# Transposes of the attention probabilities through single-pass float32 names

## The reference

```python
xn = _layernorm(x)
kv_c, q_c = xn @ W_kvd + b_kvd, xn @ W_qd + b_qd          # 64 and 192 wide
# keys and queries per head: 128 from kv_c/q_c, 64 more with a rotary embedding
scores = jnp.einsum('bhqd,bhkd->bhqk', q, k) * scale
scores = jnp.where(causal, -1e9, scores)
probs = jax.nn.softmax(scores, axis=-1)
ctx = jnp.einsum('bhqk,bhkd->bhqd', probs, values)
out = x + (ctx @ W_o + b_o) + ffn(xn)                     # ffn: one product with binarized weights
```

## Time and profile before

| | |
|---|---|
| three runs | 1427.53, 1427.95, 1428.28 us; median 1427.95 |
| the profiled execution, first to last instruction (span) | 1427.6 us |
| mean granted clock of TensorE over the span | 0.997 of full speed |
| DVE, ACT, POOL busy | 81%, 84%, 70% of the span |

### The profile page before, as it was taken

The page is one execution under the profiler, slowest core; times in us unless marked ns, Lnnn a source line. Parts: engine busy times, 40 slices in busy tenths (PEclk is TensorE's granted clock), DMA queues, the critical chain, the costliest instruction groups (busy, mean ns, idle before and its releaser), DMA issues.

```text
span 1427.6 us, 27603 instructions
## 1 busy us (share of the span) xinstructions
PE 1394.7 (98%) x9786; PEld 1262.8 (88%) x9786; DVE 1151.8 (81%) x2708; ACT 1203.2 (84%) x2603; POOL 998.3 (70%) x573
## 2 busy tenths in 40 slices
PE   6979999999999999999999999999999999999998
PEld 4769999998899999988899999999889999999987
DVE  4858898885788888887678889888677888888888
ACT  4658888997788988898788888899778988888887
POOL 6986777777667877768765777777766777666750
PEclk9999999999999999999999999999999999999999
DMA  9752212212343222211333222221233322221110
GB/s 269 226 126 50 73 50 64 64 49 64 75 106 81 79 64 64 64 44 36 78 93 96 68 68 63 64 64 49 64 75 90 87 58 65 64 63 47 36 27 31
DMA packets 46957, 106.82 MB, mean 75 GB/s; under 512 B 9333, under 2 KB 17830, under 8 KB 46822
## 3 DMA queue, kind: packets, MB, share of 16 engines
q1 hardware_dynamic: 43360, 94.01, 25.7%
q0 software_dynamic: 3296, 11.01, 2.7%
q10 hardware_dynamic: 166, 0.03, 0.0%
HBM read 48.92 MB, written 9.96 MB: 41 GB/s over the span
## 4 chain that ended last, share of the span: by engine, by line
PE 87%; ACT 6%; DVE 2%; SPq 1%; DMA 1%; POOL 1%; issue 1%; POOLq 0%; ACTq 0%; DVEq 0%
PE turn L1554 17%; PE ring L1499 11%; PE u_ps L1575 9%; PE ring L1531 9%; PE ring L1530 9%; PE u_ps L1576 9%; PE ring L1529 8%; PE o_ps L1599 4%; PE o_ps L1600 4%; PE ring L1512 2%; ACT probs L778 2%; PE ring L1438 2%; PE ring L1444 2%; ACT probs_hi L787 1%; DMA swapped<-k_rope 1%; POOL k_rope L367 1%
## 5 line engine op out<-in xcount | busy, mean ns | idle before, releaser
L1076 DVE TENSOR_SCALAR_CACHE_REDUCE probs<-ring,c_t 128x1024 f32<-128x1024 f32 (+7 forms) x512 | 414.3, 810 | 96.6 <-PE ring L1531 92.1
L1086 DVE TENSOR_TENSOR probs_lo<-turn,probs_hi 128x512 fp32r<-128x512 f32 (+1 forms) x640 | 401.2, 630 | 69.0 <-ACT probs_hi L787 64.1
L787 ACT ACTIVATE probs_hi<-turn 128x512 fp32r<-128x512 f32 (+1 forms) x640 | 349.7, 549 | 105.1 <-PE turn L1554 99.3
L778 ACT ACTIVATE probs<-probs,row_min 128x1024 f32<-128x1024 f32 (+7 forms) x512 | 394.3, 771 | 11.8 <-DVE probs L1076 9.2
L1554 PE MATMUL turn<-ident,probs 128*128 128x128 f32 x2304 | 387.2, 275 | 3.2 <-DVE probs_lo L1086 2.3
L1575 PE MATMUL u_ps<-probs_hi,kv_nat 128*128 128x256 f32 x1147 | 312.6, 302 | 1.0 <-DVE u_pair L1092 1.0
L1554 PEld LDWEIGHTS turn<-ident,probs 128*128 128x128 f32 x2304 | 282.9, 140 | 29.0 <-ACT probs L778 6.6
L1576 PE MATMUL u_ps<-probs_lo,kv_nat 128*128 128x256 f32 x1147 | 287.7, 280 | 0.0
L1529 PE MATMUL ring<-k_hi,q_hi 128*128 128x512 f32 (+3 forms) x768 | 275.4, 359 | 0.0
L1531 PE MATMUL ring<-k_hi,q_lo 128*128 128x512 f32 (+3 forms) x768 | 263.1, 343 | 0.0
L1530 PE MATMUL ring<-k_lo,q_hi 128*128 128x512 f32 (+3 forms) x768 | 262.5, 342 | 0.0
(11 more groups left out here) (229 smaller groups left out, 2582.9 us busy)
## 6 DMA issues: line engine op xcount, KB each, us to landing
swapped<-k_rope SPq DMA_DIRECT2D x128, 128.0 KB, 2.3
wv<-wv_scratch SPq DMA_DIRECT2D x62, 256.0 KB, 4.0
wp<-wp_scratch SPq DMA_DIRECT2D x62, 192.0 KB, 3.5
wp<-wp_scratch SPq DMA_DIRECT2D x31, 256.0 KB, 3.1
swapped<-q_y SPq DMA_DIRECT2D x62, 128.0 KB, 2.3
swapped<-q_x SPq DMA_DIRECT2D x62, 128.0 KB, 2.3
k_hi<-qb_kv_hi SPq DMA_DIRECT2D x16, 256.0 KB, 3.7
k_lo<-qb_kv_lo SPq DMA_DIRECT2D x16, 256.0 KB, 4.8
```

The costliest lines, as they stand in the source:

```text
L778: act.activation(p, p, ACT.Exp, scale=-1.0, bias=row_min[:, r:r + 1], accum_out=row_sum[:, g % 4, w, h:h + 1]).then_inc(exp_ready, 1)
L787: act.activation(probs_hi[:, r % 4, 0:width], turn[r % 2][:, 0:width], ACT.Identity).then_inc(turned_hi, 1)
L1076: dve.tensor_scalar(probs_of(g, w, h), ring[slot_of(entry)][:, KEY_COLUMN[qt]:KEY_COLUMN[qt] + keys], c_t[b % 2][:, qt, ds(pair * 2 + h, 1 ...
L1086: dve.tensor_tensor(probs_lo[:, r % 4, 0:width], turn[r % 2][:, 0:width], probs_hi[:, r % 4, 0:width].bitcast(F32), ALU.subtract).then_inc ...
```

## The change

The 2304 transposes at L1554 get all three operands in the single-pass float32 format. The probabilities get a second set of SBUF tensors with the same shape in that format, which lie where the first set lies: the first set is given back to the allocator at once, and the second takes its room. DVE and ACT go on writing and reading the first names, PE reads the second. The identity is made as a tensor of the single-pass format, and all its other users read a float32 view of it. The PSUM banks `turn` keep their type for ACT and DVE; the transposes write them through a view. No bytes, waits, loops or orders are changed.

```diff
-        ident, ident_bf, mask_bf = sb("ident", [P, P]), sb("ident_bf", [P, P], BF16), sb("mask_bf", [P, P], BF16)
+        ident_r, ident_bf, mask_bf = sb("ident", [P, P], F32R), sb("ident_bf", [P, P], BF16), sb("mask_bf", [P, P], BF16)
+        ident = ident_r[:, :].bitcast(F32)
...
-        probs = [[sb(f"probs{i}{h}", [P, (NT + 1) * P]) for h in range(2)] for i in range(2)]
+        with ExitStack() as plain:
+            probs = [[plain.enter_context(nc.sbuf_tensor(f"probs{i}{h}", [P, (NT + 1) * P], F32)) for h in range(2)] for i in range(2)]
+
+        probs_r = [[sb(f"probs_r{i}{h}", [P, (NT + 1) * P], F32R) for h in range(2)] for i in range(2)]
...
+        turn_r = [bank[:, :].bitcast(F32R) for bank in turn]
...
+        def probs_turned(g, w, h, kt):
+
+            long, short = LONG_SHORT[g % BLOCKS]
+            return probs_r[g % 2][h][:, ((long + 1) * w + kt) * P:][:, 0:P]
...
-            pool.affine_select(out=ident[:, :], in_=ident[:, :], compare_op=ALU.not_equal, fill=1.0, base=0,
+            pool.affine_select(out=ident_r[:, :], in_=ident_r[:, :], compare_op=ALU.not_equal, fill=1.0, base=0,
...
-                        mm = pe.transpose(turn[r % 2][:, (2 * t + h) * P:(2 * t + h + 1) * P],
-                                          probs_of(g, w, h)[:, kt * P:(kt + 1) * P], ident[:, :])
+                        mm = pe.transpose(turn_r[r % 2][:, (2 * t + h) * P:(2 * t + h + 1) * P],
+                                          probs_turned(g, w, h, kt), ident_r[:, :])
```

## The result

The changed kernel takes 1410.12 us (median of 4 runs, 1409.15 to 1411.24) against 1428.12 us (4 runs, 1427.53 to 1428.86) in the same comparison: ratio 0.9873, 95% interval 0.9859 to 0.9887. It is faster by 18 us; 62 were forecast. The profiled execution has a span of 1408.9 us, 18.7 less than before.

A forecast was written before the change was run, and what follows sets the result against it. PE was taken to bound the kernel, busy for 98% of the span. Cheaper transposes would free 122 us, less 39 for GpSimd's key chain and 21 for ACT: gain 62, time 1366 us, range 1335 to 1434.

The forecast's parts named there:

- price of the new transpose: PE's 2304 transposes at L1554: step from start to start falls from 0.108 to 0.055 us, 122 us in all.
- midway case: Transposes at 0.082 us each: PE loses 60 us; 1388 us with two thirds kept, 1408 with one third.
- tied to transposing and not to the format: Weight loads of transposes: the quick load, 140 against 189 ns, was inferred to stay in the new format, supporting 0.055 us.
- rival of the load: New-format transposes wait for weight loads, 0.110 to 0.115 us each: slower by 5 to 16 us, 1438 us; chance 0.20.
- decision point: Weight loads of the transposes: the change makes the kernel slower once a load lasts longer than 0.108 us.
- bounds 0.055 and 0.115: Limits on a new transpose's step in us: one pass from below, the single-pass format's weight load from above.
- GpSimd's key chain, 39 us lost: Chain for the next pair's keys, 12.8 of each pair's 39.8 us without slack: some 39 of 122 us lost.
- ACT as what is late next: ACT, close behind PE in the attention blocks, takes a quarter of the remaining 83 us: 21 us.
- busy floor of 181.5 us in 200: ACT in the stretch 1140 to 1340 us: 178.09 us busy plus 3.4 us of gaps, against PE falling to 180.8.
- give-back: Part of PE's 122 us lost again to other engines: 39 us to GpSimd's key chain, 21 us to ACT.
- queries' chain: GpSimd's second chain, before the scores: 4.1 us of slack against about 2.8 us gained by PE, so it holds.
- rival that the format changes nothing: Transposes at L1554 still move four bytes an element in two passes: 0 us gained, 1428 us; chance 0.15.

The follow-up runs named there:

- e9: Changed kernel with the cosine product of GpSimd's key chain done during the swap instead of after it: 1405.58 us, ratio 0.9832.
- e2: Changed kernel with GpSimd's rope operations cut to a quarter of their columns from the fourth projection on: 1406.55 us, ratio 0.9841.
- e12: Changed kernel with the fourth block's last exponential moved behind the second waiting group of the next pair: 1398.48 us, ratio 0.9779.
- e1: Separate kernel of TensorE alone, rows of 64 like instructions, nothing of the layer computed: transpose step 0.109 us old format, 0.085 new.

## Why the prediction was right in sign and wrong in size

- **The price of the new transpose** is the term that was mis-sized: taken as 0.055 us, measured as 0.085 in a row, and in groups of four as 0.091 with what the next matmul pays (the old 0.109 less 17 to 19 ns). 2304 x (0.108 - 0.055) = 122 us became 40 to 45. The prediction's own midway case, a price of 0.082, gave 1388 to 1408 us; the result is 1410.
- **How that choice was made.** The old step was right (0.108 against 0.1095), and so, it seems, was the one pass: the shortest new transposes last 222 ns. The inference from load durations, "tied to transposing and not to the format", held for the duration, which stays at 140, and failed for what it was used for: in the old format a load really is over in 0.063 us or less (L186), and the new one holds the load path for 0.085 under the same duration, although its matmul starts 0.03 us after the load. The sum needed the interval between two loads' starts, and no row of before had it for this format.
- **The rival of the load** named the right mechanism, a load that outlasts the pass, with the wrong number: 0.110 to 0.115, from score matmuls, would have made it slower. The decision point, 0.108, was right; 0.085 is under it. The bounds 0.055 and 0.115 held.
- **GpSimd's key chain, 39 us lost:** failed. e9 and e2 shorten it by 2.4 and 5 us and leave the pair at 39.2. "No slack" was read from ACT taking the result at once; whether an engine had to wait was not in that row. No wait at k_hi appeared in plain pairs.
- **ACT as what is late next:** right in kind, too small in size. It wasn't the busy floor of 181.5 us in 200 that bit, since PE's stream only fell to about 193 or 194 of 200 (362 x 0.017 to 0.0195 = 6.2 to 7.1). It was one place, the start of a pair, where an exponent, an evacuation and a rounding stand in a row; elsewhere ACT idled for PE. e12 moved one 0.7 us instruction from there and gained 13 us.
- **The two errors of the give-back nearly cancelled, by luck:** 51% kept was forecast, 42 to 47% came (18.7 of 40 to 45). With the right price and the forecast's share the time would have been 1428 less 20 to 23, 1405 to 1408 us.
- **Right:** the queries' chain held, no wait at the scores came for it; the load's row stayed near 140; L1564 stands at 10% of the chain for 9 forecast; waits for probs_lo and the probabilities came at the transposes. ACT's share was to rise above 87%; it is 85%. A group of four was to take 0.39 us; it takes 0.46, where it took 0.60. The rival that the format changes nothing fell with the duration of 244 ns.

## What to carry to other kernels

Price an instruction by the distance from its start to that of the next of its kind, for the load path as for the array, and measure it when the format is new, in a row of like instructions and then in the group in which it stands: a duration row doesn't show what is held, and the row of like instructions leaves out what the next instruction of another kind pays. When one engine gets faster, look for the one place in the period where its partner's work stands in a row without a gap; the average share of busy time misses it, and moving one instruction there can be worth as much as the change itself. A chain whose result is used at once is a bound only if its user had nothing else to do: shorten it in an experiment before charging time to it.

## What was not expected of the hardware

- The load durations, 140 and 141 ns, are the same for float32 and single-pass float32 transposes, and the loads hold the path for 0.063 us or less and for 0.085.
- With 64 rows, so 64 moving columns, the new format is the slower one: the steps of the old and the new row in e1 are 4.0 / 63 = 0.063 us and 0.085.

```profile
L186 PE MATMUL bank<-ident_r,data_r x64: 220/223/273, 48.3 to 52.3; 64*128 64x64 f32 x64
...
L189 PE MATMUL bank<-ident_r,data_r x64: 245/248/313, 53.5 to 59.2; 64*128 64x64 f32 x64
...
L192 PE MATMUL bank<-ident_r,data_r x64: 272/273/422, 61.3 to 70.0; 128*64 128x128 f32 x64
...
L195 PE MATMUL bank<-ident_r,data_r x64: 220/224/228, 71.1 to 74.9; 128*64 128x128 f32 x64
```

 The old format's step fell with the moving columns (0.109 to 0.063), the new one's didn't (0.085 both times). With 64 weight columns the new one takes 3.8 / 63 = 0.060 (L195), the old one 0.109 as before (L192, its part at the full clock). In these rows the new format's step follows the weights, the old one's the moving data. The quotients of L189 and L192, 0.090 and 0.138, hold instructions at half the clock: the last seven steps of L189 are 0.127 us, and the first of L192 0.213.
- The granted clock fell to 0.50 from 58.3 to 65.1 us in e1, while PE was busy without a gap. Before the fall PE had done a row of bf16 matmuls of 128 columns, then two rows of transposes with 64 moving columns; through the rows of transposes with 128 it had stayed at 1.00. It rose again within the transposes of L192. No run here tests what decides it.

```profile
58.00:59.00 1.00, 1.00 (x12) 1.00 (x10) 0.00 (x0) 0.00 (x0) 0.65 0.00 0
59.00:60.00 1.00, 1.00 (x6) 0.84 (x6) 0.00 (x0) 0.00 (x0) 0.50 0.07 16
...
65.00:66.00 1.00, 1.00 (x10) 0.96 (x9) 0.00 (x0) 0.00 (x0) 0.93 0.00 0
```

- A matmul behind a new transpose starts 0.09 to 0.1 us after it, behind an old one 0.03.
